# Attention's rows of maxima in two loads placed ahead of later groups' loads, QKV's row loads placed ahead of its stores, routing's picks in two parts

## What is computed

```python
x = x + 0.5 * ffn(layernorm(x))        # twice: ahead of attention and behind it
x = x + attn(layernorm(x))
def ffn(x):                            # E = 8 experts, top 2, mean of relu(x @ W_e + b_e)
    logits = x @ W_gate + b_gate
    _, top_idx = top_k(logits, 2)
    y_all = relu(einsum('bsd,edh->bseh', x, W_e) + b_e)
    return take_along_axis(y_all, top_idx[..., None], axis=2).mean(axis=2)
def attn(x):                           # 4 sequences of 512, 32 heads of 16
    q, k, v = split(clip(x @ Wqkv.T, -8, 8))
    q, k = layer_norm(q, w, b), layer_norm(k, w, b)
    scores = q @ k.T / 4 + slope[h] * (pos_k - pos_q), causal
    return softmax(scores) @ v @ Wout.T
```

## Time and profile before

| | |
|---|---|
| median of 3 runs | 975.37 us (970.96 to 982.41) |
| profiled execution | 983.81 us, of it span 982.0 us |
| PE, DVE, ACT, POOL busy | 86%, 64%, 46%, 46% of the span |
| mean granted PE clock | 0.923 |
| DMA | 164.5 MB, 168 GB/s over the span |
| QKV 350 to 400 us | DMA share 0.98, 233 GB/s |
| attention 491 to 595 us | DMA share 0.69, 149 GB/s, clock 1.00 |
| attention 595 to 680 us | DMA share 0.96, 184 GB/s, clock 0.96 |

### The profile page before, as it was taken

One profiled execution on the slowest core, in us unless ns is written; L12 is line 12 of the kernel. 1 busy time (PEld: TensorE's weight loads), 2 busy tenths in 40 slices (PEclk: granted clock), 3 DMA queues, 4 the chain that ended last, 5 costly groups with the idle time before them and its releaser, 6 DMA issues. The chain is left out here.

```text
span 982.0 us, 18936 instructions
## 1 busy us (share of the span) xinstructions
PE 841.5 (86%) x5922; PEld 592.5 (60%) x5923; DVE 632.4 (64%) x1289; ACT 449.1 (46%) x834; POOL 446.1 (45%) x565
## 2 busy tenths in 40 slices
PE   3666999993989998878899999889989983899995
PEld 1344888872677777655455555445557752788874
DVE  7966344333978877776688887678728768344432
ACT  3541333332244443347577777577754430233331
POOL 7732677764022222224243344235446431577764
PEclk9785999996899999978899999899999995899998
DMA  9985677863264689665667679898239940578874
GB/s 341 387 300 175 124 148 145 149 118 53 54 197 150 196 199 230 195 196 127 146 139 154 143 154 189 165 192 178 54 107 321 323 161 32 123 144 152 149 133 62
DMA packets 113255, 164.54 MB, mean 168 GB/s; under 512 B 16929, under 2 KB 74401, under 8 KB 112897
## 3 DMA queue, kind: packets, MB, share of 16 engines
q1 hardware_dynamic: 95328, 126.40, 46.6%
q0 software_dynamic: 17856, 37.25, 20.4%
HBM read 100.05 MB, written 68.68 MB: 172 GB/s over the span
## 5 line engine op out<-in xcount | busy, mean ns | idle before, releaser
L901 DVE TENSOR_REDUCE att_part<-att_s_ps 128x2 f32<-128x1024 f32 (+2 forms) x160 | 195.2, 1225 | 46.4 <-PE att_s_ps L733 42.4
L858 ACT ACTIVATE att_prob<-att_st_ps 128x512 f32<-128x512 f32 x320 | 174.2, 598 | 75.3 <-PE att_st_ps L758 71.2
L687 POOL TENSOR_SCALAR_AFFINE_SELECT att_prob<-att_prob 128x256 f32<-128x256 f32 (+1 forms) x224 | 93.7, 442 | 108.0 <-ACT att_prob L858 107.9
L153 PE MATMUL exp_z_ps<-ex_w_hi,exp_xT_hi 128*128 x312 | 132.4, 424 | 1.7 <-issue 1.3
L155 PE MATMUL exp_z_ps<-ex_w_hi,exp_xT_lo 128*128 x312 | 124.8, 400 | 0.0
L154 PE MATMUL exp_z_ps<-ex_w_lo,exp_xT_hi 128*128 x312 | 124.7, 400 | 0.0
L1684 ACT ACTIVATE exp_y<-exp_y 128x512 f32<-128x512 f32 x72 | 45.5, 632 | 170.5 <-DVE exp_y L1703 142.0
L1691 DVE TENSOR_TENSOR exp_xT_lo<-exp_t_ps,exp_xT_hi 128x512 fp32r<-128x512 f32 x78 | 53.9, 692 | 99.8 <-ACT exp_xT_hi L1675 81.2
L1263 POOL TENSOR_TENSOR ex_w_lo<-ex_w_lo,ex_w_hi 128x1024 fp32r<-128x1024 f32 x32 | 77.0, 2418 | 78.0 <-ACT ex_w_hi L1404 41.6
L771 PE MATMUL att_pv_ps<-att_prob,att_v_sb 128*32 128x256 f32 (+2 forms) x1280 | 103.2, 397 | 1.6 <-ACT wt_w_turned L863 1.6
L153 PE MATMUL qkv_o_ps<-qkv_w_hi,qkv_xT_hi 128*128 128x512 f32 x192 | 82.6, 430 | 2.4 <-DVE qkv_xT_lo L464 1.6
(11 more groups left out here) (206 smaller groups left out, 1618.2 us busy)
## 6 DMA issues: line engine op xcount, KB each, us to landing
ex_w_lo<-in_L_ffn_W_e SPq DMA_DIRECT2D x32, 512.0 KB, 6.7
v_vals<-st_vals SPq DMA_DIRECT2D x16, 512.0 KB, 2.9
q_parts<-st_partq SPq DMA_DIRECT2D x32, 256.0 KB, 3.6
k_parts<-st_partk SPq DMA_DIRECT2D x32, 256.0 KB, 4.0
att_v_sb<-v_vals SPq DMA_DIRECT2D x32, 256.0 KB, 3.8
ex_bias<-in_L_attn_hidden_states SPq DMA_DIRECT2D x8, 512.0 KB, 7.4
acc<-ex_bias SPq DMA_DIRECT2D x8, 512.0 KB, 8.3
xn<-ex_rows SPq DMA_DIRECT2D x8, 512.0 KB, 5.5
```

The costliest lines, as they stand in the source:

```text
L153: nc.tensor.matmul(out, x_hi[:, s], w_hi(c), start=(c == 0), stop=False)
L687: last = nc.gpsimd.affine_select(out=block, in_=block, compare_op=ALU.is_ge, fill=0.0, base=0, pattern=[[0, block.shape[1]], [1, P]], chan ...
L858: nc.scalar.activation(prob[n % 2][:, col:col + 512], st_ps[(e + half) % 3][:, :], ACT.Exp).then_inc(exp_done, 1)
L901: nc.vector.tensor_reduce(out, src, X_AXIS, ALU.max, negate=True).then_inc(red_done, 1)
```

## The change

- QKV: in SP's `step`, `load_x(t + 3)` comes ahead of `store_qk(t - 2)`.
- Attention: the parts of the maxima are laid out by half, so that one DMA per half carries four rows of `m_rows` into two rows of the stack: two DMAs of 8 KB in place of four of 4 KB, and `m_loaded` counts 32 per group in place of 64. In SP's loop `max_rows(n + 1)` comes first, ahead of the stack's and the values' loads.
- Routing: once 7 of 8 pairs are there, DVE copies the logits of 14 tiles out of PSUM and picks for them; when the last pair is there it picks for the last 2 tiles. PE turns the logits of pair 6 ahead of the transposes of pair 7, and turns those of pair 7 only when the copy is done. The buffer for the turned logits gets a place of its own, shared with a later one.

```diff
             def step(t, par):
+                if not (isinstance(t, int) and t + 3 >= TILES):
+                    load_x(t + 3, 1 - par)
                 if after(t, 2):
                     store_qk(t - 2, par)
-                if not (isinstance(t, int) and t + 3 >= TILES):
-                    load_x(t + 3, 1 - par)
                 store_v(t, par)
...
             def max_rows(n):
                 sp.wait_ge(m_rows_done, n + 1)
                 for half, base in halves():
-                    for part_of in range(2):
-                        row = base + SCORE_ROWS + part_of
-                        src = m_rows[n % 2][4 * part_of + 2 * half:4 * part_of + 2 * half + 2, :]
-                        sp.dma_start(q_st[n % SLOTS][row:row + 1, :, :].bitcast(F32), src.bitcast(F32)).then_inc(m_loaded[n % 2], 16)
+                    row = base + SCORE_ROWS
+                    src = m_rows[n % 2][HG * half:HG * (half + 1), :]
+                    sp.dma_start(q_st[n % SLOTS][row:row + MAX_ROWS, :, :].bitcast(F32), src.bitcast(F32)).then_inc(m_loaded[n % 2], 16)
...
             for n in range(NG):
+
+                if n + 1 < NG:
+                    max_rows(n + 1)
                 if n + AHEAD < SLOTS:
                     st.load_fixed(sp, n + AHEAD)
                 if n + AHEAD < NG:
                     load(n + AHEAD)
                 if n + 2 < NG:
                     load_v(n + 2)
-                if n + 1 < NG:
-                    max_rows(n + 1)
...
+            if u == PAIRS:
+
+                turn_logits(u - 2)
             if 1 <= u <= PAIRS:
                 transpose(2 * u - 2)
                 transpose(2 * u - 1)
-            if u >= 2:
+            if u >= 2 and u != PAIRS:
+                if u == PAIRS + 1:
+                    pe.wait_ge(lg_kept, 1)
                 turn_logits(u - 2)
...
+        def picks(t0, t1, first):
+            n, three = slice(t0, t1), [P, t1 - t0, E]
+            for k, source in enumerate((first, rest)):
+                chain(nc.vector.tensor_reduce(best[:, n, 0], source[:, n, :], X_AXIS, ALU.max))
+                chain(nc.vector.tensor_tensor(eq[:, n, :], source[:, n, :], best[:, n, :].to_broadcast(three), ALU.is_equal))
...
+        dve.wait_ge(gate_done, PAIRS - 1)
+        nc.vector.tensor_copy(kept[:, 0:TILES - 2, :], logits[:, 0:TILES - 2, :]).then_inc(lg_kept, 1)
+        dve.wait_ge(lg_kept, 1)
+        picks(0, TILES - 2, kept)
         dve.wait_ge(gate_done, PAIRS)
...
+        picks(TILES - 2, TILES, logits)
```

More of the change, by code:

```diff
@@ L581, in attention_block @@
         part = [m.sb(f"part{i}", [P, 2, 2, SEGS]) for i in range(2)]
-        m_parts = [m.sb(f"m_parts{i}", [P, 2, 4, SEGS], F32R) for i in range(2)]
+        m_parts = [m.sb(f"m_parts{i}", [P, 2, 2, 2, SEGS], F32R) for i in range(2)]
         m_rows = [m.sb(f"m_rows{i}", [2 * HG, SEQ], F32R) for i in range(2)]
@@ L668, in split_max @@
                 at_least(pool, mT_done, n - 1)
[L669 to L670 removed]
+                whole, parts = part[n % 2][:, :, :, :], m_parts[n % 2]
+                nc.gpsimd.tensor_copy(parts[:, :, 0, :, :], whole).then_inc(m_hi_done, 1)
                 pool.wait_ge(m_hi_done, n + 1)
[L672 removed]
+                nc.gpsimd.tensor_tensor(parts[:, :, 1, :, :], whole, parts[:, :, 0, :, :].bitcast(F32),
                                         ALU.subtract).then_inc(m_lo_done, 1)
@@ L741, in turn_max @@
                 for i, seg in enumerate((0, 4, 6, 5)):
-                    last = nc.tensor.matmul(bank[0:2 * HG, i * P:(i + 1) * P], m_parts[n % 2][:, :, :, seg], ident_r[:, :],
+                    last = nc.tensor.matmul(bank[0:2 * HG, i * P:(i + 1) * P], m_parts[n % 2][:, :, :, :, seg].rearrange("p a k b -> p (a k b)"), ident_r[:, :],
                                             start=True, stop=True)
@@ L1489, in vector @@
         dve.wait_ge(const_done, 12)
-        dve.wait_ge(gate_done, PAIRS)
[L1491 to L1498, removed]
-                chain(nc.vector.scalar_tensor_tensor(rest[:, :, :], pick[0][:, :, :], NEG, logits[:, :, :], ALU.mult, ALU.add))
@@ L1503, in vector @@
-        chain(nc.vector.tensor_tensor(picked[:, :, :], pick[0][:, :, :], pick[1][:, :, :], ALU.add))
-        chain(nc.vector.scalar_tensor_tensor(val[:, :, :], picked[:, :, :], -100.0, n_expert[:, :, :], ALU.mult, ALU.add))
-        chain(nc.vector.tensor_reduce(low[:, :, 0], val[:, :, :], X_AXIS, ALU.min))
-        chain(nc.vector.tensor_tensor(pair[:, :, 0, :], val[:, :, :], low[:, :, :].to_broadcast(three), ALU.is_equal))
-        nc.vector.tensor_tensor(pair[:, :, 1, :], picked[:, :, :], pair[:, :, 0, :], ALU.subtract).then_inc(picked_done, 1)
+        kept = over[:, :, :].rearrange("p e t -> p (e t)").rearrange("p (t e) -> p t e", e=E)
@@ new lines, in picks @@
+        def picks(t0, t1, first):
[3 more added lines that the diff above has]
+                chain(nc.vector.tensor_tensor(eq[:, n, :], source[:, n, :], best[:, n, :].to_broadcast(three), ALU.is_equal))
+                chain(nc.vector.scalar_tensor_tensor(val[:, n, :], eq[:, n, :], -100.0, n_expert[:, n, :], ALU.mult, ALU.add))
+                chain(nc.vector.tensor_reduce(low[:, n, 0], val[:, n, :], X_AXIS, ALU.min))
+                chain(nc.vector.tensor_tensor(pick[k][:, n, :], val[:, n, :], low[:, n, :].to_broadcast(three), ALU.is_equal))
+                if k == 0:
+                    chain(nc.vector.scalar_tensor_tensor(rest[:, n, :], pick[0][:, n, :], NEG, first[:, n, :], ALU.mult, ALU.add))
+            chain(nc.vector.tensor_tensor(picked[:, n, :], pick[0][:, n, :], pick[1][:, n, :], ALU.add))
+            chain(nc.vector.scalar_tensor_tensor(val[:, n, :], picked[:, n, :], -100.0, n_expert[:, n, :], ALU.mult, ALU.add))
+            chain(nc.vector.tensor_reduce(low[:, n, 0], val[:, n, :], X_AXIS, ALU.min))
+            chain(nc.vector.tensor_tensor(pair[:, n, 0, :], val[:, n, :], low[:, n, :].to_broadcast(three), ALU.is_equal))
+            nc.vector.tensor_tensor(pair[:, n, 1, :], picked[:, n, :], pair[:, n, 0, :], ALU.subtract).then_inc(picked_done, 1)
```

15 lines of the change are left out of this document (9 added, 6 removed).

## The result

The changed kernel takes 972.05 us (median of 20 runs, 961.3 to 977.78), the kernel before, run beside it, 979.76 us (20 runs). The ratio is 0.9912, with a 95% interval of 0.9884 to 0.994: 8.6 us (5.9 to 11.4) are gained, a little under 1%. Forecast were 16 us from a median of 975.37, so 959.4 us. The profiled span went from 982.0 to 974.0 us.

| stretch | before, us | after, us | difference |
|---|---|---|---|
| start to the first rank product | 68.9 | 69.4 | +0.5 |
| to QKV's first statistics of x two tiles ahead (DVE) | 186.2 | 190.0 | +3.7 |
| to attention's first copy of maxima (ACT) | 181.9 | 182.9 | +1.0 |
| to its last copy of maxima | 273.9 | 264.0 | -9.9 |
| to the second rank product | 104.9 | 102.1 | -2.8 |

A forecast was written before the change was run, and what follows sets the result against it. PE, busy 86% of the span, was held up by waits in QKV, attention and routing; 9.5 + 7.7 + 2.3 = 19.5 us, taken as 16 from the median, gave 959.4 us, range 953 to 965.

The forecast's parts named there:

- 9.5 us: QKV: giving out x ahead of four stores gains 7.1 us in four loaded steps and 2.44 at 286.62; range 5.5 to 11.9.
- the middle, 4.6 us: QKV: assumed landing time of x in its new place, between 3.6 and 5.6 us; four steps then take 44.2 us.
- The sign I had named for being wrong: Profile after: x landing after more than 5.5 us, or PE's first scores waiting for stacks, would prove the forecast wrong.
- The stores come at most half a microsecond later: QKV: stores passed by x are delayed by at most half a microsecond, with a step's time until ACT needs their buffers.
- 6.46 us: QKV: SP's time from v's store to give out the group's loads and reach x; step spacing was this plus x's landing.
- Attention, 7.7 us: Attention: two maxima loads for four gain 4.8 us in the first stretch and 2.9 in the second; range 3 to 11.2.
- SP keeps up: Attention's first stretch: SP's work per group falls from 8.9 to 7.7 us, below the 8.26 us of a group.
- Picks, 2.3 us: Routing: splitting the picks gains 0.4 us in routing 1 and 1.95 in routing 2; range 0.5 to 2.8.
- The DMA engines are the bound: Rival, 20%: x lands after 5.6 us, attention's second stretch gains nothing, the first 3 us; 9 us from the median, 966.4.
- the waits only move: Rival, 7%: PE, DVE and SP are close behind; only routing and the place at 286.62 gain, 4.7 us: 970.7.
- The stacks did not come too late: Rival, 3%: attention's stacks, now given out behind the maxima, land too late; the kernel ends slower, about 996 us.
- The discount: Whole kernel: 19.5 us for the profiled execution, 8.4 us above the median, taken as 16 us from the median.

The follow-up runs named there:

- qkv_alone: Kernel before with only QKV's edit, x given out ahead of the four stores of q and k: ratio 1.001.
- picks_alone: Kernel before with only routing's edit, the picks in two parts: ratio 0.9995.
- before_copy_late: Kernel before with the copy of the bias rows behind the fifth gather: ratio 0.9953.
- picks_copy_late: Kernel before with the picks in two parts and the copy of the bias rows behind the fifth gather: ratio 0.9919.
- groups_behind_qkv: Changed kernel with only group 0's loads left in QKV, those of groups 1 to 3 behind QKV's last stores: 979.18 us in one run.
- att_alone: Kernel before with only attention's edit, two loads of maxima rows for four, ahead of the later groups' loads: ratio 0.9944.
- experiment 3: Kernel before with two loads of maxima rows in the old place, ratio 0.9973, or four ahead of the later group's loads, ratio 1.0017.
- half_groups: Changed kernel with QKV's last eight steps each giving out half a group's loads, instead of four giving out a whole group's: ratio 0.9831.
- copy_late: Changed kernel with the copy of the bias rows waiting until the fifth gather has landed: ratio 0.9893.

## Why the prediction was wrong

By terms, in the traces: QKV was forecast at 9.5 us and gave 1.1, attention at 7.7 and gave 7.3, the picks at 2.3 and gave 1.1 in the second routing and nothing that can be told in the first; experts 1 had no term and lost 4.

- **What bounds QKV**: right in what waits (DVE for x), wrong in why. "What is ahead of it is 1 MB of loads given out over 6 us rather than 1 MB of stores in 2.4 us" was taken for an advantage. The failed step is the term of **9.5 us**: the landing of "the middle, 4.6 us" measured 5.5, 8.4, 7.5 and 6.3 us, all but one outside the bounds of 3.6 to 5.6. I had bounded a landing in a new place by landings in old ones, in queues that held other things. The sign I had named for being wrong, x landing after more than 5.5 us, is what the profile shows.
- **"The stores come at most half a microsecond later"**: true of their issue in the first loaded step (0.46 us), not of their landing (up to 9.1 us for k, 6.0 before), so ACT waits 9.1 us where it had waited for none. And SP's hold-up at x (2.03 us where an issue takes 0.42) got no new place in the sum; it passed to v's store and grew to 4.83 us. The "6.46 us" from v's store to x, on which the spacing rested, became 7.6, 11.0 and 9.9 us (361.32 to 368.93 and so on). Of the 9.5 us only the place at 286 us came (2.4 us), and the loaded steps gave 1.3 of it back.
- **Attention, 7.7 us**: right in the traces. Over the executions with the old attention (before, qkv_alone, picks_alone, before_copy_late, picks_copy_late) its copies span 268.6 us on average, over nine with both edits 261.3: 7.3 us (groups_behind_qkv is left out, since its attention starts with an 11 us wait). By the ratio of att_alone it is 5.5 us (1.3 to 9.8). Copies 0 to 7: 65.4 to 60.8 us, 4.6 for the 4.8 forecast. Copies 19 to 31: 103.5 to 101.4 us, 2.1 for 2.9, where single executions range from 99.1 (twelve groups of 8.26 with no wait) to 107.0; the one profile of before was the worst of them; with such a spread the 2.1 us aren't told from none. That the number of issues and not their place gives the gain in the first stretch is shown by experiment 3. "SP keeps up" went too far: in eight of the nine the rows of group 5 still leave 1.6 to 3.1 us behind their copy, and in five PE waits 0.4 to 1.1 us for them.
- **Picks, 2.3 us**: in routing 2 the path from norm to rank product is 9.58 us in five executions without the edit at the full clock and 8.45 in seven with it: 1.1 us. The 1.95 us forecast belong to a gate product at half clock, as in the earlier trace rows: there it is 10.9 to 11.2 us without and 9.2 to 9.3 with. Right for that execution, but the lower of two clock levels (5 of 17 executions) was taken for the rule. In routing 1 the path ranges from 9.6 to 12.5 us without the edit and from 8.4 to 13.3 with it; the 0.5 us between the two first profiles says nothing.
- **What was not in the sum**: experts 1. What would now come out sooner was looked for in QKV and attention only, not for POOL's gathers and SP's copy. The copy that left too early took 4 us in the traces, more than the picks gave.
- **The rivals**: "The DMA engines are the bound", 966.4 us, came nearest in what is gained (9 us forecast, 8.6 measured; by the median alone, 972.05, "the waits only move" with 970.7 is nearer, as before itself was measured 4 us higher this time). Its first clause (x lands after 5.6 us or more) is what happened, but its 5.5 us in QKV came to 1.1 and its 3 us in attention to 7.3, so the near number is luck. Its reading of the share fell with half_groups: 230 GB/s at a share of 0.98 and no wait (350 to 390 us), against 233 GB/s at 0.98 before (350 to 400 us). "The waits only move" named the mechanism. The stacks did not come too late: no wait of the first scores for them.
- **The discount** from 19.5 to 16 was in the right direction: before's profiled attention was 5.3 us above the mean of its kind.

## What to carry to other kernels

When a transfer is late, count what is given out in the step as a whole before changing its order: in this kernel one order only passed the hold-up on and gained nothing, another gained 8 us and left the stores late, and halving each step's loads removed both, for 11 us in the traces and 8 to 11 by the ratios. A hold-up of the issuing engine belongs to the place in the traffic, not to the DMA whose row shows it. And where a stage gets quicker, look for transfers of other queues that were just late enough: 0.6 us in the start of one copy cost 4 us here.

## What the runs showed of the hardware that I had not expected

- A DMA issue on SP that mostly takes 0.3 to 0.45 us took up to 4.87 us (v's store, copy_late) behind fourteen loads and five other DMAs, and held up all behind it; behind seven loads and the same five it took 0.35 us.
- The DMA share is no measure of work: 0.72 and 0.63 for the same 153 GB/s, by the order of issue alone; two stretches at 0.97 and 0.99 held no wait for a transfer.
- Beside a DRAM to DRAM copy on SP's queue, which landed after 8.6 to 9.7 us, PE got the rows of one of POOL's gathers only 0.2 to 1.5 us behind the copy's landing. It was the second where the copy was given out up to 0.49 us behind that gather's start, the third where it was 0.65 us or more.
- TensorE's granted clock rising within one group of 16 transposes (0.50 to 0.63 on average over it) moved an SP issue by 0.6 us, and that decided the race above.
